# A pre-norm decoder layer on one core: seven of the eight transposes ahead of the feed-forward part move from TensorE to 32x32 block transposes on VectorE

## The reference

```python
x = x + _L0_attn_ref(_layernorm(x), W_qkv, W_out, b_out)          # blocks of 128 rows, one head, causal
x = x + _L0_xattn_ref(_layernorm(x), ctx, ctx, mask, ...)         # 16 heads, silu instead of softmax
x = x + _L0_ffn_ref(_layernorm(x), w1, b1, w2, b2)

def _L0_ffn_ref(x, w1, b1, w2, b2):
    h = gelu(einsum('bse,eh->bsh', x, w1) + b1)                   # 512 -> 2048
    return einsum('bsh,he->bse', h, w2) + b2                      # 2048 -> 512

def _layernorm(x, eps=1e-05):
    return (x - mean(x)) / sqrt(var(x) + eps)
```

## Time and profile before

| | us |
|---|---|
| median of three runs | 1313.33 |
| lowest and highest | 1313.2, 1313.77 |
| span of the profiled execution (first to last instruction) | 1312.2 |
| feed-forward section in it, from about | 585 |
| PE busy | 1289.4 (98% of the span) |
| DVE busy | 585.1 (45%) |
| ACT busy | 488.4 (37%) |
| POOL busy | 244.2 (19%) |

### The profile page before, as it was taken

The page is one execution under the profiler, slowest core; times in us unless marked ns, Lnnn a source line. Parts: engine busy times, 40 slices in busy tenths (PEclk is TensorE's granted clock), DMA queues, the critical chain, the costliest instruction groups (busy, mean ns, idle before and its releaser), DMA issues.

```text
span 1312.2 us, 15758 instructions
## 1 busy us (share of the span) xinstructions
PE 1289.4 (98%) x5897; PEld 1046.8 (80%) x5897; DVE 585.1 (45%) x1098; ACT 488.4 (37%) x887; POOL 244.2 (19%) x225
## 2 busy tenths in 40 slices
PE   9989999999999999999999999999999999999999
PEld 7877878787878788767888888888888888888887
DVE  7475768585858585845522222222312211222211
ACT  6254554545454555443322222222222222222221
POOL 1303232313141414138500100100102001001000
PEclk9998999999999999999999999999999999999999
DMA  8220202020202020316210010010010100100000
GB/s 288 73 72 0 85 1 84 1 85 0 84 0 84 0 84 4 116 42 208 64 65 0 0 65 1 0 64 0 25 39 0 64 0 0 64 0 0 32 0 32
DMA packets 40486, 60.04 MB, mean 46 GB/s; under 512 B 4224, under 2 KB 14464, under 8 KB 40448
## 3 DMA queue, kind: packets, MB, share of 16 engines
q1 hardware_dynamic: 40448, 59.53, 13.6%
HBM read 41.17 MB, written 18.35 MB: 45 GB/s over the span
## 4 chain that ended last, share of the span: by engine, by line
PE 54%; DMA 1%; DVE 0%; SPq 0%; ACT 0%; issue 0%; DVEq 0%
PE bank L50 18%; PE bank L51 18%; PE bank L49 18%; PE bank L140 1%; DMA w_raw<-in_w 0%; DMA x_dram<-resid 0%; DVE resid L1129 0%; SPq L1026 0%; DVE w_parts L184 0%; ACT w_parts L180 0%; SPq L1024 0%; SPq L1023 0%; SPq L188 0%; DVEq L1128 0%; SPq L1033 0%
## 5 line engine op out<-in xcount | busy, mean ns | idle before, releaser
L1121 DVE TENSOR_TENSOR hid_lo<-gelu_out,hid_hi 128x512 fp32r<-128x512 f32 x128 | 97.0, 758 | 493.7 <-ACT gelu_out L1097 493.7
L49 PE MATMUL bank<-zT,w_parts 128*128 128x512 f32 x768 | 300.9, 392 | 5.3 <-DVE zT L149 1.8
L51 PE MATMUL bank<-zT,w_parts 128*128 128x512 f32 x768 | 301.1, 392 | 0.0
L50 PE MATMUL bank<-zT,w_parts 128*128 128x512 f32 x768 | 301.0, 392 | 0.0
L1093 ACT ACTIVATE hid_hi<-bank,b_col 128x512 fp32r<-128x512 f32 x128 | 88.0, 688 | 484.4 <-PE bank L51 484.4
L49 PE MATMUL bank<-w2p_hi,hid_lo 128*128 128x512 f32 x512 | 203.8, 398 | 0.7 <-DVE hid_lo L1121 0.7
L50 PE MATMUL bank<-w2p_lo,hid_hi 128*128 128x512 f32 x512 | 202.5, 395 | 0.0
L51 PE MATMUL bank<-w2p_hi,hid_hi 128*128 128x512 f32 x512 | 202.4, 395 | 0.0
L49 PEld LDWEIGHTS bank<-zT,w_parts 128*128 128x128 f32 x768 | 145.1, 189 | 39.5 <-issue 3.0
L50 PEld LDWEIGHTS bank<-zT,w_parts 128*128 128x128 f32 x768 | 144.8, 189 | 32.1
L51 PEld LDWEIGHTS bank<-zT,w_parts 128*128 128x128 f32 x768 | 144.8, 189 | 31.0
(11 more groups left out here) (138 smaller groups left out, 1816.6 us busy)
## 6 DMA issues: line engine op xcount, KB each, us to landing
x_in<-in_x SPq DMA_DIRECT2D x32, 256.0 KB, 3.4
x_dram<-resid SPq DMA_DIRECT2D x32, 256.0 KB, 2.1
w_raw<-in_w SPq DMA_DIRECT2D x32, 256.0 KB, 3.4
resid<-x_dram SPq DMA_DIRECT2D x32, 256.0 KB, 3.1
out_dram<-resid SPq DMA_DIRECT2D x32, 256.0 KB, 2.1
resid<-in_wqkvT SPq DMA_DIRECT2D x12, 256.0 KB, 4.2
mask_i<-in_mask SPq DMA_DIRECT2D x16, 128.0 KB, 2.6
values_now<-values_dram SPq DMA_DIRECT2D x8, 256.0 KB, 2.8
```

The source lines that it names most:

```text
L49: pe.matmul(out_ap, lhs[1], rhs[0], start=start, stop=False)
L50: pe.matmul(out_ap, lhs[0], rhs[1], start=False, stop=False)
L51: return pe.matmul(out_ap, lhs[0], rhs[0], start=False, stop=stop)
L1121: dve.tensor_tensor(hid[1][:, c % 4, :], gelu_out[:, c % 2, :], f(hid[0][:, c % 4, :]), ALU.subtract).then_inc(hid_lo, 1)
```

## The change

After the change, the rows of tiles 1 to 7 are turned by VectorE. VectorE's transpose turns blocks of 32x32 within its 32 partitions and can write to another group of 32 partitions. One instruction `squares(n)` takes 32 partitions of `zn` (`row`), and in all four blocks i and all four feature groups the 32 features of group `col`: 512 elements in each of 32 partitions, 16 blocks. It writes them to the 32 partitions `col` of a new buffer `z3_cols`, 8 KB for each partition. Sixteen instructions turn a tile.

They stand at chunks c = 8 to 15 of tile t, two in each, ahead of that chunk's `hid_lo`. The statistics move from c = 8 to c = 4 (c = 6 in tile 0) and the normalised rows from c = 12 to c = 8. In tile 0 `norm_rstd` of GpSimd moves from behind the last `split_w2` to behind `split_w2(8)`. After the last Gelu, ScalarE waits for all 16 transposes and copies `z3_cols` to the high part of `zT`, four copies; VectorE makes the low part from `z3_cols`, four subtractions. TensorE has no transposes left in this section. The build is given `dynamic_dma_scratch_size=4096`, which it was not before.

```diff
@@ vector: buffers and the squares
+            z3_cols = sb("z3_cols", [P, EC, TILE])
...
+            QUADS = P // SQUARE
+            TURNS = QUADS * QUADS
+            FIRST_TURN, TURNS_AT_ONCE = 8, 2
+
+            def squares(n):
+                row, col = divmod(n, QUADS)
+                taken = zn[cols(row, SQUARE), :, :].rearrange("p i (c q f) -> p i c q f", c=EC, q=QUADS)
+                put = z3_cols[cols(col, SQUARE), :, :].rearrange("p c (i q t) -> p i c q t", i=NB, q=QUADS)
+                return put[:, :, :, row, :], taken[:, :, :, col, :]
@@ gpsimd
+                                if c == FIRST_TURN:
+                                    norm_rstd(pool, mv3, ve3, rstd3, ln3, 1)
+                        elif more:
+                            norm_rstd(pool, mv3, ve3, rstd3, ln3, t + 1)
                         if more:
-                            norm_rstd(pool, mv3, ve3, rstd3, ln3, t + 1)
                             add_bias(t + 1, 1 - par)
@@ scalar
                         if more:
-                            for i in range(NB):
-                                transpose_high(act, i, LN3_BANK[i], z3T_done, z3T_hi, t + 1)
+                            act.wait_ge(z3_turned, TURNS * (t + 1))
+                            for c in range(EC):
+                                act.activation(zT[0][:, c, :], z3_cols[:, c, :], ACT.Copy).then_inc(z3T_hi, 1)
@@ vector
-                            if c == 8 and more:
+                            if c == (6 if splits_weights(t) else 4) and more:
...
-                            if c == 12 and more:
-                                dve.wait_ge(z3T_done, NB * (t + 1))
+                            if c == FIRST_TURN and more:
+                                if splits_weights(t):
+                                    dve.wait_ge(z3T_done, NB)
                                 norm_rows(dve, lambda i: resid[:, 1 - par, i, :], mv3, rstd3, ln3, t + 1)
+                                dve.wait_ge(z3_ready, NB * (t + 2))
+                                dve.wait_ge(z3T_hi, NB * (t + 1))
+                                dve.nop(nofuse=True)
+                            if c >= FIRST_TURN and more:
+                                for n in range(TURNS_AT_ONCE):
+                                    dve.transpose(*squares(TURNS_AT_ONCE * (c - FIRST_TURN) + n)
+                                                  ).then_inc(z3_turned, 1)
...
                         if more:
-                            for i in range(NB):
-                                transpose_low(dve, i, LN3_BANK[i], z3T_hi, z3T_lo, t + 1)
+                            for c in range(EC):
+                                dve.wait_ge(z3T_hi, EC * (t + 1) + c + 1)
+                                dve.tensor_tensor(zT[1][:, c, :], z3_cols[:, c, :], f(zT[0][:, c, :]), ALU.subtract
+                                                  ).then_inc(z3T_lo, 1)
@@ tensor
-                        if more:
-                            next_rows(t, 0)
-                            pe.wait_ge(hid_full, FC * t + FC - 2)
-                            next_rows(t, 1)
-                            pe.wait_ge(hid_full, FC * t + FC - 1)
-                            next_rows(t, 2)
                         down(t, FC - 2)
-                        if more:
-                            pe.wait_ge(hid_full, FC * (t + 1))
-                            next_rows(t, 3)
                         down(t, FC - 1)
@@ launch
-    nc = bacc.Bacc("TRN2", target_bir_lowering=False, num_devices=1)
+    nc = bacc.Bacc("TRN2", target_bir_lowering=False, num_devices=1, dynamic_dma_scratch_size=4096)
```

More of the change, by code:

```diff
@@ L24 @@
 STAGES = 3
+SQUARE = 32
 VALUE_BANK = (1, 2, 3, 4)
@@ L37 @@
 FIRST_BANK = (4, 5, 6, 7)
-LN3_BANK = (7, 5, 6, 4)
 def decoder_layer_program(nc, x, ctxT, mask, wqkvT, woutT, b_out, xwqT, bq, xwkT, bk, xwvT, bv, xwoT,
@@ L1004, in decoder_layer_program @@
             down_done, rows_done = sem("down_done"), sem("rows_done")
+            z3_turned = sem("z3_turned")
             DOWNS = FC - 1
+            QUADS = P // SQUARE
[6 more added lines that the diff above has]
+                return put[:, :, :, row, :], taken[:, :, :, col, :]
             def feed_tiles(engine, step):
@@ L1158, in down @@
                             last.then_inc(down_done, 1)
-                    def next_rows(t, i):
-                        transposed_rows(pe, z3_ready, t + 1, i, LN3_BANK[i], z3T_done)
                     def step(t, more, par):
```

## The result

| | before | after |
|---|---|---|
| median, us | 1313.26 (4 runs, 1312.19 to 1313.77) | 1299.62 (4 runs, 1298.13 to 1300.65) |
| ratio | | 0.9897, 95% interval 0.9884 to 0.991 |
| span of the profiled execution, us | 1312.2 | 1298.4 |

The kernel is 13.6 us faster. The prediction was 1301.1 us, by 12.25 us of transposes taken from TensorE, with a range down to 1299.8. In later comparisons the medians were 12.6 and 9.9 us apart, and 12.28 us when most of the scatter between executions had been removed.

What follows compares the result with a forecast made beforehand. PE's instruction list was taken to bound the feed-forward section. Removing 112 transposes, 7 tiles at 1.75 us, takes 12.25 us off the 1313.33 us median, with VectorE's work hidden: 1301.1 us, range 1299.8 to 1303.0.

Steps and rivals of the forecast that it cites:

- What bounds the kernel: From tile 0's start to the last residual addition, PE's list sets the time; PE busy 98% of 1312.2 us.
- The price on PE: Feed-forward tiles: 16 transposes cost PE 1.75 us a tile by distance of starts, 109 ns each; 12.25 us in seven tiles.
- the fourth rival: PE's transposes cost their 272 ns duration each: 30.5 us saved, 1282.9 us; chance 0.01.
- The price on VectorE: Each block transpose of 32 partitions by 512 elements takes 0.7 us (0.54 to 1.79); 78 us more work.
- Room and margins: Two transposes and hid_lo take 2.1 us of a 5.54 us chunk; at the tile's end margins are 3.4 and 3.3 us.
- Every margin above is more than 3 us: Support for the rival that all VectorE work is hidden, forecast 1301.1 us; chance 0.86.
- everything at its upper bound: Tile 0, chunk 8: with zn at 2.2 us and other passes at 1.79, w1_low(11) ends at 636.3; margin 6 us.
- Its own range: Whole kernel, all-hidden case: 1299.8 to 1303.0 us, from run spread 0.6 us and chip difference of a microsecond; chance 0.86.
- The median of the runs lies 1.1 us above the span: Whole kernel: span 1312.2 less 12.25 gives 1299.95 us; median 1313.33 less 12.25 gives 1301.1 us.
- the cover: VectorE's 78 us of added transposes are hidden behind PE's matmuls, so PE never waits for them.
- the two limits: PE waits beyond 2.49 us for each VectorE transpose (rival chance 0.05), or beyond 3.3 us at a tile's end (0.06).

Runs made afterwards that it cites:

- later comparisons: Unaltered changed kernel measured again against the kernel before: 1300.34 us, ratio 0.9907; then 1301.36 us, ratio 0.9912; with two PE pauses filled in both kernels, 1297.61 against 1309.89 us.
- the tripled one: Changed kernel with each pair of VectorE transposes run three times in all tiles: 1305.18 us, ratio 0.9945 to the kernel before.
- the filling: Discarded or repeated matmuls put into PE's two longest attention pauses: changed kernel 1298.07 and 1297.61 us, kernel before 1309.89 us.

## Why the prediction was off, point by point

- *What bounds the kernel*: right. PE's list sets the time; taking 112 transposes out gave their distance, putting them back took it away again (ratio 0.9997), and doubling them cost it once more. One window was set wrong: tile 0 begins at 584.3, not 587, so it took 93.3 us. No term rested on that.
- *The price on PE*, 1.75 us a tile: right. Tiles of the loop shortened from 90.43 to 88.69 us, and with most of the scatter removed the difference is 12.28 us. The distance of starts is the price, not the 272 ns of duration that the fourth rival took. The figure of the Trainium skill (TensorE: Matmul & The Clock Gate, Part 4: PE-mode transpose), about 275 ns, is such a duration; it agrees with the 272 ns of the earlier trace rows.
- *The price on VectorE*, 0.7 us: measured 703 ns. The Trainium skill (Vector Engine (DVE) Microarchitecture Reference, 3.8 The reshape front-end and per-opcode configuration) says that the transpose is pipelined to one element per cycle and lane. The trace is in line with that: 703 ns for 512 elements in each lane, beside 0.69 us for a `hid_lo` of the same length. VectorE as a whole is busy for 667 us, 4 more than stated; 2.5 of them are the rows `zn` in tile 0.
- *Room and margins*: right where it counted. 3.7 us at the end of the tile for 3.4 predicted; with 5.8 us of transposes moved there PE waited 2.8 us a tile, as worked out. "Every margin above is more than 3 us" was not so: at the upper bound a chunk has 5.4 us of work in 5.54. In tile 0 the bound held, but the rows `zn` took 4.45 us beside GpSimd, in the changed kernel as in the tripled one, not the 2.2 us that the prediction used for them with "everything at its upper bound".
- *The step that failed*: "Its own range is 1299.8 to 1303.0 us: the runs spread by 0.6 us ... and a chip may differ by a microsecond." The mechanism and the 12.25 us were right; the term for the scatter was mis-sized. The spread of three runs, 0.6 us, was taken for the spread of executions. That is 5 us for the changed kernel and up to 6.7 for the one before on one chip, and most of it comes from whether and how long PE's clock falls behind pauses in the attention part; a median of four moves by a microsecond or more. The prediction looked at the clock in the feed-forward section alone. The page of before showed more, in a row that stands below this list. A range of 1298.5 to 1303.5 would have been honest, an estimate from that spread of 5 us.
- *Also wrong*: "The median of the runs lies 1.1 us above the span". In every later execution of the kernel before and of the changed one the device time is 2.2 to 2.3 us above the span (the profiled one after: 1300.65 and 1298.4); with PE's transposes put back it is up to 2.5. By that the profiled execution of before took some 1314.5 us, more than any of the three runs: it was one of the longer ones, with 6.8 us of half clock near 100 us. The sum was not touched, since the difference was taken from the median, but the gap should have said that the runs shown were not all there is.

The row is that of the granted clock in 40 equal slices of the span, in tenths of full speed (9 is 90% or more). The 8 is the slice from 98 to 131 us:

```profile
PEclk9998999999999999999999999999999999999999
```

Shown by experiment: the price, the cover, the two limits, the cause of most of the scatter. Not separated: how the first measurement's extra 1.4 us divides between the clock and the landing of loads in the setup and in tile 0 (about 0.5 us each in the one pair of traces). Part of it was luck of the draw: all four executions of the changed kernel had a clock of 0.997 or 0.998 there, while three of six and three of five had 0.995 or 0.996 in the two later comparisons.

## What to carry to other kernels

On an engine that never pauses, a moved instruction is worth the distance between starts, and the receiving engine's price is its deadline, not its busy share: VectorE took 78 us for nothing, and in the loop would take 34 us a tile for nothing, but 5.8 us in the wrong place of each tile cost 30. Before giving a range, look for places where the bounding engine pauses anywhere in the program and where its clock falls behind them: they, not the few runs shown, say how far executions lie apart. A pause that can't be removed may be worth filling with work that is thrown away.

## What was not expected of the hardware

- Of thirteen traces without the filling, eleven have 3.4 or 6.8 us at 1.2 GHz behind PE's pauses of 1.2 to 1.9 us near 100 us, nine have it behind the pause of 2.9 us near 553 us, and five have 3.4 us of it behind the pause of 1.8 us near 83 us; one has none. Executions of the kernel before differed by up to 6.7 us on one chip, with mean clocks from 0.993 to 1.000. With the two larger pauses filled the changed kernel's lay within 0.8 us, and nine of eleven of the kernel before within 1.6.
- A wait of PE for a late engine can cost more than itself: 19.8 us of waits became 30 us, and 45.3 became 67.
- Block transposes on VectorE took 699 to 710 ns with no outlier, in tile 0 beside a busy GpSimd too, where one-input passes `zn` of 128x512 went from 1.9 us for four to 4.45.
